# Routing steps, row copies and two evictions put in another order in a fused four-layer attention kernel

## The reference

```python
logits = jnp.einsum('nd,ed->ne', xf, gate_w)
topk_vals, topk_idx = jax.lax.top_k(logits, K)          # K = 2
topk_gates = jax.nn.softmax(topk_vals, axis=-1)
h = jax.nn.silu(jnp.einsum('nd,ehd->neh', xf, exp_w1))
eo = jnp.einsum('neh,edh->ned', h, exp_w2)
sel = jnp.einsum('ned,ne->nd', eo, gates)               # gates: zero but for the two chosen
return sh + sel                                          # sh: the shared expert; h + this at the call
```

## Time and profile before

| | us |
|---|---|
| median of three runs | 661.26 (660.8 to 661.41) |
| the profiled execution | 660.79 |
| its span in the trace | 658.9 |

### The profile page before, as it was taken

One profiled execution on the slowest core, in us unless ns is written; L12 is line 12 of the kernel. 1 busy time (PEld: TensorE's weight loads), 2 busy tenths in 40 slices (PEclk: granted clock), 3 DMA queues, 4 the chain that ended last, 5 costly groups with the idle time before them and its releaser, 6 DMA issues.

```text
span 658.9 us, 24223 instructions
## 1 busy us (share of the span) xinstructions
PE 583.2 (89%) x8126; PEld 431.9 (66%) x8126; DVE 503.7 (76%) x1210; ACT 481.6 (73%) x1355; POOL 405.6 (62%) x625
## 2 busy tenths in 40 slices
PE   6888888999999889998887769999996988888895
PEld 3556565777777656666555526999993655566663
DVE  2998999888898888889888833344425999988993
ACT  3678888899999888888767533545534778888994
POOL 5667766788888755565688772355562677764220
PEclk9999999999999999999989879999997999999997
DMA  7434433322455300100111011122224000000110
GB/s 211 136 93 95 107 78 82 78 63 66 124 133 156 99 26 25 33 27 26 35 37 40 27 36 54 43 64 70 65 80 109 26 27 26 23 18 19 37 31 26
DMA packets 49663, 42.04 MB, mean 64 GB/s; under 512 B 6409, under 2 KB 44173, under 8 KB 48544
## 3 DMA queue, kind: packets, MB, share of 16 engines
q1 hardware_dynamic: 41392, 23.13, 12.6%
q10 hardware_dynamic: 5904, 13.45, 8.7%
q0 software_dynamic: 2272, 4.24, 2.0%
HBM read 25.41 MB, written 14.79 MB: 61 GB/s over the span
## 4 chain that ended last, share of the span: by engine, by line
PE 29%; issue 16%; POOL 9%; DVE 6%; ACT 4%; DMA 1%; POOLq 0%; DVEq 0%; ACTq 0%
PE ps L882 5%; PE ps L871 5%; POOL k_by_j L525 4%; PE ps L643 3%; PE ps L800 2%; POOL sorted_rows L548 2%; PE ps L834 2%; DVE inv L1197 2%; PE ps L844 2%; PE ps L676 2%; DVE prob L1235 2%; PE ps L811 1%; PE ps L666 1%; DMA mow<-expert_out 1%; PE ps L698 1%
## 5 line engine op out<-in xcount | busy, mean ns | idle before, releaser
L525 POOL TENSOR_TENSOR k_by_j<-k_t,cst 128x1024 f32<-128x1024 f32 (+1 forms) x96 | 168.4, 1754 | 46.1 <-ACT k_t L960 29.3
L1066 ACT ACTIVATE prob<-prob 128x1024 f32<-128x1024 f32 (+1 forms) x96 | 95.0, 989 | 32.0 <-DVE prob L1235 31.4
L1223 DVE TENSOR_REDUCE top<-ps 128x16 f32<-128x1024 f32 (+1 forms) x96 | 108.3, 1128 | 9.4 <-PE ps L643 9.1
L676 PEld LDWEIGHTS ps<-cst,prob 128*128 128x128 f32 x704 | 77.8, 143 | 56.2 <-ACT prob L1066 39.5
L1235 DVE TENSOR_TENSOR prob<-ps,top 128x1024 f32<-128x1024 f32 (+1 forms) x96 | 108.1, 1126 | 0.7
L1197 DVE RECIPROCAL inv<-ps 128x128 f32<-128x128 f32 x96 | 91.6, 954 | 19.3 <-PE ps L811 16.2
L498 POOL TENSOR_TENSOR rstd<-spread,half_neg 128x1 f32<-128x1 f32 x80 | 45.1, 564 | 93.1 <-DVE spread L1314 51.7
L643 PE MATMUL ps<-k_by_j,q_t 64*64 64x512 f32 (+1 forms) x768 | 100.3, 593 | 0.2
L676 PE MATMUL ps<-cst,prob 128*128 128x128 f32 x704 | 97.8, 281 | 2.7 <-ACT prob L1066 2.6
L800 PE MATMUL ps<-prob_t,v 128*32 128x64 f32 x2816 | 59.9, 223 | 31.8 <-ACT x_t L1044 15.0
L800 PEld LDWEIGHTS ps<-prob_t,v 128*32 128x32 f32 x2816 | 46.3, 110 | 54.5 <-issue 54.5
(11 more groups left out here) (162 smaller groups left out, 1241.3 us busy)
## 6 DMA issues: line engine op xcount, KB each, us to landing
sorted_rows<-zero_rows ACTq DMA_DIRECT2D x32, 276.2 KB, 2.7
stage_m<-in_m SPq DMA_DIRECT2D x80, 64.0 KB
mow<-in_mow SPq DMA_DIRECT2D x18, 256.0 KB, 3.0
stage_kv<-in_ctx_t SPq DMA_DIRECT2D x64, 64.0 KB
rows_in<-sorted_rows SPq DMA_DIRECT2D x39, 65.0 KB, 1.8
...
```

Of the source, the lines that this page charges most:

```text
L525: pool.tensor_tensor(k_by_j[:, p, 0:nj, :], k_t[:, p:p + 1, :].broadcast_to([128, nj, TOK]), cst[:, cj:cj + nj].unsqueeze(2).broadcast_to( ...
L676: mm = pe.transpose(ps[:, 2 * p + half, k * 128:(k + 1) * 128], prob[:, p, q * 128:(q + 1) * 128], ident)
L1066: act.activation(prob[:, p, 0:w], prob[:, p, 0:w], ACT.Exp, scale=float(D // heads(pr)) ** -0.5).then_inc(exp_d, 1)
L1223: dve.tensor_reduce(top[:, p, 0:nh].rearrange("p (b h) -> p b h", b=2), sc, AX.X, ALU.max).then_inc(top_d, 1)
```

## The change

Six edits, none of which changes what is computed.

1. **POOL, routing marks first.** `chosen` and `taken` (L534, L537) stood behind `k_by_j` in a slot; they now stand ahead of the XT step.
2. **No copy of the sum in RO.** DVE's residual sum in phase 3 is written to `x_tok` itself (`kept(pair)`), and POOL's copy `x_tok<-y` (L482) is gone there, 16 instructions. ACT's L1092 and DVE's L1317 read `x_tok`. `res_d` is not counted in phase 3 any more; `RES_BEFORE` and the waits are renumbered (`wait_res`).
3. **PE and DVE, rank first.** PE's rank matmuls (L689, L690) move from behind to ahead of the eight turns L676. DVE's `rank` (L1246) moves from behind the subtraction L1235 to ahead of the maximum L1223.
4. **ACT, turned rows first.** `q_t` and `k_t` stood ahead of the copies into `x_t` (L1032, L1044/L1046, and `n_f` L1041 in RO); now they stand behind them. This holds in all phases.
5. **POOL, feed-forward root first.** `rstd_f` (L491) moves from behind the XT step to the head of the slot.
6. **POOL, negated mean first.** In the layer norm `minus` (L501) moves ahead of `rstd` (L498).

```diff
@@ POOL slot
+                pr = follows(at, OFF_FY, FF)
+                    pool.tensor_tensor(rstd_f[:, pr.p, :], spread_f[:, pr.p, :], half_neg[:, :], ALU.pow)
...
+                pr = follows(at, OFF_R2, RO)
+                    wait_own(pool, r_h, pr)
+                    wait_own(pool, r_p, pr, 2)
+                    pool.tensor_tensor(chosen[:, p, :], hot[:, i, 0, :], hot[:, i, 1, :], ALU.add).then_inc(r_c, 1)
+                    wait_own(pool, r_c, pr)
+                    wait_own(pool, r_t, pr, 1)
+                    pool.tensor_tensor(taken[:, i + 1, :], taken[:, i, :], chosen[:, p, :], ALU.add).then_inc(r_t, 1)
...
                 elif pr is not None and POST[pr.phase] == "rms":
-                    wait_pair(pool, y_d, pr, 0, apart=True)
-                    pool.tensor_copy(x_tok[:, pr.i, :], y[:, pr.p, :]).then_inc(res_d, 1)
                     if pr.phase == RO:
                         wait_pair(pool, norm_d, pr)
                         pool.tensor_copy(token_rows[:, pr.i, 1, 0:D], token_rows[:, pr.i, 0, 0:D]).then_inc(r_two, 1)
+                    else:
+                        wait_pair(pool, y_d, pr, 0, apart=True)
+                        pool.tensor_copy(x_tok[:, pr.i, :], y[:, pr.p, :]).then_inc(res_d, 1)
...
                 pr = at(OFF_OUT)
+                    if POST[pr.phase] == "ln":
+                        wait_pair(pool, agg_d, pr)
+                        wait_pair(pool, shift_d, pr, 2)
+                        pool.tensor_tensor(minus[:, p, :], none[:, :], moments[:, p, 0:1], ALU.subtract).then_inc(minus_d, 1)
                     wait_pair(pool, spread_d, pr)
                     wait_pair(pool, norm_d, pr, 2)
                     pool.tensor_tensor(rstd[:, p, :], spread[:, p, :], half_neg[:, :], ALU.pow)
@@ ACT slot: this block now behind the copies into x_t
+                pr = at(OFF_PROJ)
+                    wait_pair(act, proj_d, pr)
+                    wait_pair(act, score_d, pr, 2)
+                    project(pr, 0, q_t, q_e)
+                    project(pr, 1, k_t, k_e)
@@ DVE slot
+                pr = follows(at, OFF_RP, RO)
+                    wait_own(dve, r_p, pr)
+                    wait_own(dve, r_m, pr, 2)
+                    dve.tensor_tensor(rank[:, pr.p, :], ps[:, B_F, 256:256 + E], base, ALU.add).then_inc(r_k, 1)
                 pr = at(OFF_SCORE)
...
-                    dve.tensor_tensor(y[:, p, :], ps[:, B_OUT, OUT], x_tok[:, pr.i, :], ALU.add).then_inc(y_d, 1)
+                    dve.tensor_tensor(kept(pr), ps[:, B_OUT, OUT], x_tok[:, pr.i, :], ALU.add).then_inc(y_d, 1)
```

More of the change, by code:

```diff
@@ L321, in wait_own, with wait_res, kept @@
             (wait_apart if apart else lambda e, *x: e.wait_ge(*x))(eng, sem_, pr.i + (1 - back))
+        def wait_res(eng, pair, back=0):
+            n = RES_BEFORE[pair.phase] + pair.i - back + 1
+            if not (isinstance(n, int) and n <= 0):
+                eng.wait_ge(res_d, n)
+        def kept(pair):
+            return x_tok[:, pair.i, :] if pair.phase == RO else y[:, pair.p, :]
         def own_ones(pair, k):
@@ L474, in slot @@
                     wait_pair(pool, norm_d, pr)
-                    if not (isinstance(pr.n, int) and pr.n == 0):
-                        pool.wait_ge(res_d, pr.n)
+                    wait_res(pool, pr, 1)
                     pool.tensor_tensor(scaled[:, p, :], normed[:, p, :], g, ALU.mult).then_inc(gsc_d, 1)
@@ L499, in slot @@
                         .then_inc(rstd_d, 1)
-                    if POST[pr.phase] == "ln":
-                        pool.tensor_tensor(minus[:, p, :], none[:, :], moments[:, p, 0:1], ALU.subtract).then_inc(minus_d, 1)
-                    else:
-                        pool.sem_inc(minus_d, 1)
                     if POST[pr.phase] == "ln":
@@ L527, in slot @@
                         .then_inc(kj_d, 1)
-                pr = follows(at, OFF_R2, RO)
-                if pr is not None:
-                    p, i = pr.p, pr.i
-                    wait_own(pool, r_h, pr)
-                    wait_own(pool, r_p, pr, 2)
-                    pool.tensor_tensor(chosen[:, p, :], hot[:, i, 0, :], hot[:, i, 1, :], ALU.add).then_inc(r_c, 1)
-                    wait_own(pool, r_c, pr)
-                    wait_own(pool, r_t, pr, 1)
-                    pool.tensor_tensor(taken[:, i + 1, :], taken[:, i, :], chosen[:, p, :], ALU.add).then_inc(r_t, 1)
                 pr = follows(at, OFF_RS, RO)
@@ L667, in slot @@
                         .then_inc(l_acc, 1)
-                pr = at(OFF_PV)
-                if pr is not None:
-                    p, npr = pr.p, heads(pr) // 2
-                    wait_pair(pe, exp_d, pr)
-                    for half, done in enumerate((pt0_d, pt1_d)):
-                        for k in range(npr // 2):
-                            q = half * (npr // 2) + k
-                            mm = pe.transpose(ps[:, 2 * p + half, k * 128:(k + 1) * 128],
-                                              prob[:, p, q * 128:(q + 1) * 128], ident)
-                        mm.then_inc(done, 1)
                 pr = follows(at, OFF_RP, RO)
@@ L691, in slot @@
                         .then_inc(r_p, 1)
+                pr = at(OFF_PV)
+                if pr is not None:
+                    p, npr = pr.p, heads(pr) // 2
+                    wait_pair(pe, exp_d, pr)
+                    for half, done in enumerate((pt0_d, pt1_d)):
+                        for k in range(npr // 2):
+                            q = half * (npr // 2) + k
+                            mm = pe.transpose(ps[:, 2 * p + half, k * 128:(k + 1) * 128],
+                                              prob[:, p, q * 128:(q + 1) * 128], ident)
+                        mm.then_inc(done, 1)
                 pr = at(OFF_V)
@@ L1241, in slot @@
                 one, two, three = follows(at, OFF_R1, RO), follows(at, OFF_R2, RO), follows(at, OFF_RP, RO)
-                if three is not None:
-                    r = three.p
-                    wait_own(dve, r_p, three)
-                    wait_own(dve, r_m, three, 2)
-                    dve.tensor_tensor(rank[:, r, :], ps[:, B_F, 256:256 + E], base, ALU.add).then_inc(r_k, 1)
                 if two is not None:
@@ L1254, in slot @@
                 if three is not None:
+                    r = three.p
                     wait_own(dve, r_k, three)
@@ L1300, in slot @@
                             dve.wait_ge(res_d, RES_BEFORE[ph - 1] + 1 + pr.i)
[L1301 to L1303 removed]
+                    if POST[ph] != "none" and ph != RO:
+                        wait_res(dve, pr, 2)
+                    dve.tensor_tensor(kept(pr), ps[:, B_OUT, OUT], x_tok[:, pr.i, :], ALU.add).then_inc(y_d, 1)
                 pr = at(OFF_OUT)
@@ L1420, in _ @@
             run_slots(dve, GROUPS[1], slot, {2 * k - 1: lambda k=k: combine(k) for k in range(1, NP // 2)})
-RES_BEFORE = [NP * sum(k != "none" for k in POST[:n]) for n in range(len(POST))]
+RES_BEFORE = [NP * sum(k != "none" for m, k in enumerate(POST[:n]) if m != RO) for n in range(len(POST))]
 def constants():
```

44 lines of the change are left out of this document (21 added, 23 removed).

## The result

The change makes the kernel faster: 642.72 us (median of 4 runs, 640.19 to 644.33) against 661.03 us for the kernel before on the same chip. The ratio is 0.9751, 95% interval 0.9718 to 0.9784. The forecast was 651.4 (646.5 to 657.5): right in direction, 8.7 us too small a gain. The profiled execution took 642.99, its span is 641.1.

What follows compares the result with a forecast made beforehand. Limits differ by stage: POOL for routing with transfers, PE for feed-forward, loops of engines elsewhere. Gains 4.6 + 2.6 + 2.2 + 0.5 = 9.9 us gave 650.9, plus 0.47 for the run median: 651.4 us, range 646.5 to 657.5.

Steps and rivals of the forecast that it cites:

- "Edit 1 only moves `chosen` and `taken`, and adds or saves nothing on POOL": Routed slots with transfers: moving the marks costs POOL nothing but ends PE's 1.0 us wait, helping reach 6.03 us throughout.
- Edit 2: POOL's slots in phase 3: dropping the copy saves 0.23 us each, taking the transfer slot from 6.26 to 6.03.
- Edit 3: Two routed slots before transfers: the rank wait is on the path; 0.4 us each, 0.8 in all.
- Edit 4 before routing: Phases 2 and 3 before routing: ACT's `x_t` begins 0.2 us earlier; 13 x 0.2 = 2.6 us gained.
- Phase 5: Earlier `x_t` against later `k_t`: between 4.1 us lost and 4.0 gained, taken as 0.5 us gained over 11 slots.
- The new loop: In phase 5, `inv`, division, turn, `x_t`, `q_t`, `k_t`, `k_by_j`, `inv`: claimed about as long as a slot now takes.
- rival B: Phase 5: `k_by_j` comes later and DVE's L1324 always waits behind it; 4.1 us lost, 656.0 us; chance 0.12.
- Edit 6: Layer norm on POOL, phases 0 and 4: `shift_n` needs only the end of `rstd`; 17 x 0.13 = 2.2 us gained.
- Feed-forward and seam at nothing: PE sets the feed-forward stage, so 0 was taken, with ends of +3.2 and -1 us; the seam got no term.
- routing and drain: Phase 3: 2.9 us from transfer slots, 0.8 from routed slots before them, 0.9 from four emptying slots; together 4.6.
- Rival C: More than forecast: phase 5 gains 3.1 us, feed-forward 1, phase 0 1.4 more; 646.4 us; chance 0.12.
- E: Slower: ACT stands at `x_t` until the turn is done; feed-forward loses 14.8 us, phase 5 4.6; 670.8 us; chance 0.06.

## Why the prediction was wrong, step by step

- **"Edit 1 only moves `chosen` and `taken`, and adds or saves nothing on POOL"**: this step failed, and 4.9 of the 7.9 us that the sum lacks are in its term. The prediction saw the gap of 0.56 us in the earlier trace rows and took it as part of the transfer. It belonged to `taken`'s wait. With it closed, the slots are 5.7 instead of 6.03, and the drain is shorter as well: 9.5 us off from start 53 to 64, where the term was 4.6. Edit 1 alone gave 2.5 in the slots and 1.8 in the drain. That it "takes PE's wait of 1.0 away" was nearly right: 0.3 is left. But `chosen` is not "a whole slot early", it is 3.1 us early.
- **Edit 2**, 0.23 us a slot: right, 0.27 measured. Slots of 6.03 appear when edits 1 and 3 are away.
- **Edit 3**, 0.8 us in the two slots before the transfers: right in the slots (without edit 3 each is 0.4 longer). What was missed is that the sum treated edits 1 and 3 as separate terms. Edit 3 alone costs 11 us.
- **Edit 4 before routing**, 13 x 0.2: right, 11 x 0.19 in the stretch measured.
- **Phase 5**, a gain of 0.05 us a slot as "a value near the middle" of +4.1 and -4.0: failed. In the 11 slots that the term speaks of (starts 84 to 95) the gain was 0.20 us a slot, 2.2 in all. The 3.6 us from start 78 on hold another 0.6 in the first slots and 0.7 in the end of the program, which varies by more than that between the traces. The new loop (`k_t` behind `x_t`, then `k_by_j`, then `inv`) assumed that `k_by_j` still begins ahead of the sum. It doesn't; the sum slips in before it, and `inv` waits for PE alone. The rule of the Trainium skill on the shared ports ("SBUF — State Buffer", section "Who interferes with whom"), which the prediction put beside rival B, agrees with the rows (0.28 us begun before, 1.04 begun inside). But here it worked the other way: `k_by_j` starts 1.01 us behind the start of DVE's subtraction (604.92 to 605.93), where it was 0.86 before (614.09 to 614.95), and the sum goes ahead of it.
- **Edit 6**, 17 x 0.13 = 2.2 us: over-sized. `shift_n` follows `rstd` by 0.70 us (89.68 to 90.38) where the term had 0.65 and the earlier trace rows 0.78. It is 0.09 us a slot, 1.0 in phase 4; in phase 0 nothing is left of it. The rows fit a gain eaten by `neg_m` meeting `scaled`, which no run tests by itself. The forecast that DVE stands only behind `k_by_j` there missed the second POOL instruction.
- **Feed-forward and seam at nothing**: 0.7 and 0.4 us of gain. The 0.4 is edit 4's. Of the 0.7, edit 5 makes 0.3; the stretch takes 118.55 to 118.61 us in three other kernels with the old code there, so the rest is within what varies.

Terms forecast against found: routing and drain 4.6, 9.5; edit 4 before routing 2.6, 2.1; edit 6 2.2, 1.0; phase 5 0.5, 3.6; uncounted 0, 1.6 (0.5 of it loading, which is chance). 9.9 against 17.8. Rival C had the right direction, but its reasons give only 646.4: its phase 5 came near, its full gain in phase 0 did not come, and the routing slots were not among its reasons. B did not occur, since the sum no longer waits behind `k_by_j`. E did not occur: the feed-forward stage is not longer. What could have slowed the kernel was edit 3 without edit 1, which no rival names.

What stays open: the drain varies by 1.6 us between kernels with like code there, and the stretch from start 64 to 68 by up to 4, so the routing term is known only to 1 or 2 us. The slots of phase 3 with transfers are known to 0.1.
